# Ten normalisations in a fused eight-layer kernel: one reciprocal-root instruction per normalisation, and four of sixteen tiles moved from VectorE to ScalarE

## The reference

```python
def _layernorm(x, axis=-1, eps=1e-05):
    m = jnp.mean(x, axis=axis, keepdims=True)
    v = jnp.var(x, axis=axis, keepdims=True)
    return (x - m) / jnp.sqrt(v + eps)

x = x + _L0_attn_a_ref(_layernorm(x, axis=-1), ...)
x = x + _L0_ffn_ref(_layernorm(x, axis=-1), ...)
x = x + _L0_attn_b_ref(_layernorm(x, axis=-1), ...)
x = x + _L0_ffn_ref(_layernorm(x, axis=-1), ...)
x = x + _L1_attn_a_ref(_layernorm(x, axis=-1), ...)
x = x + _L1_ffn_ref(_layernorm(x, axis=-1), ...)
x = x + _L1_attn_b_ref(_layernorm(x, axis=-1), ...)
x = x + _L1_ffn_ref(_layernorm(x, axis=-1), ...)
```

## Time and profile before

| | |
|---|---|
| time, median of 3 runs | 1395.28 us (1394.18 to 1395.79) |
| the profiled execution's own time | 1395.96 us |
| its span, first to last instruction | 1394.1 us |
| PE busy (matmul) | 1048.9 us, 75% |
| DVE busy | 949.0 us, 68% |
| ACT busy | 509.3 us, 37% |
| POOL busy | 376.2 us, 27% |
| mean granted TensorE clock | 0.869 of full speed |

### The profile page before, as it was taken

The page is one execution under the profiler, slowest core; times in us unless marked ns, Lnnn a source line. Parts: engine busy times, 40 slices in busy tenths (PEclk is TensorE's granted clock), DMA queues, the critical chain, the costliest instruction groups (busy, mean ns, idle before and its releaser), DMA issues. The chain is left out here.

```text
span 1394.1 us, 17853 instructions
## 1 busy us (share of the span) xinstructions
PE 1048.9 (75%) x5802; PEld 544.4 (39%) x5802; DVE 949.0 (68%) x1953; ACT 509.3 (37%) x1034; POOL 376.2 (27%) x357
## 2 busy tenths in 40 slices
PE   4245999997599999957865766539994867539994
PEld 2112333343233333334544421316663444416663
DVE  6755998762699877447998799653336899653335
ACT  2403566776056677733101310103333411103333
POOL 2610000100100010012444344215662444415662
PEclk9657999999799999978995898559997887559997
DMA  3481000004400000271220111101112121001113
GB/s 93 112 93 26 2 1 1 1 2 69 71 2 1 1 1 2 31 203 41 68 61 0 39 46 53 30 12 36 41 45 78 38 65 33 22 21 35 43 43 110
DMA packets 43533, 58.24 MB, mean 42 GB/s; under 512 B 7630, under 2 KB 25878, under 8 KB 43438
## 3 DMA queue, kind: packets, MB, share of 16 engines
q1 hardware_dynamic: 38446, 46.79, 14.8%
q0 software_dynamic: 4992, 10.23, 2.6%
HBM read 42.95 MB, written 13.76 MB: 41 GB/s over the span
## 5 line engine op out<-in xcount | busy, mean ns | idle before, releaser
L578 DVE TENSOR_REDUCE mpart<-ps 128x1 f32<-128x512 f32 (+3 forms) x640 | 349.5, 603 | 114.8 <-PE ps L612 58.3
L674 ACT ACTIVATE arena<-ps 128x512 f32<-128x512 f32 (+3 forms) x640 | 296.2, 541 | 239.8 <-PE ps L630 163.8
L612 PE MATMUL ps<-arena 128*128 128x512 bf16 (+3 forms) x640 | 225.8, 365 | 49.9 <-PEq L388 18.3
L627 PE MATMUL ps<-arena 128*128 128x512 bf16 (+3 forms) x640 | 201.4, 350 | 14.1 <-DMA arena<-mrow 13.8
L910 POOL TENSOR_TENSOR arena<-arena 128x512 f32<-128x512 f32 x96 | 122.2, 1273 | 165.3 <-DVE arena L963 165.3
L612 PEld LDWEIGHTS ps<-arena 128*128 128x128 bf16 x640 | 62.3, 98 | 230.7 <-DVE mpart L578 146.6
L642 PE MATMUL ps<-arena,w 128*32 128x512 f32 (+3 forms) x1280 | 150.8, 543 | 0.4 <-ACT w L682 0.4
L1502 ACT ACTIVATE arena<-ps 128x512 f32<-128x512 f32 x78 | 46.6, 597 | 218.9 <-PE ps L1565 148.0
L1412 DVE COPY arena<-ps 128x128 f32<-128x128 f32 x78 | 22.8, 292 | 149.5 <-PE ps L1555 149.5
L949 DVE TENSOR_TENSOR arena<-arena 128x512 f32<-128x512 f32 x62 | 102.4, 1651 | 12.0 <-ACT arena L1016 4.6
L172 POOL TENSOR_TENSOR small<-small,neghalf 128x4 f32<-128x4 f32 x44 | 47.4, 1112 | 220.7 <-DVE small L159 220.7
(11 more groups left out here) (242 smaller groups left out, 1544.6 us busy)
## 6 DMA issues: line engine op xcount, KB each, us to landing
arena<-q_parts SPq DMA_DIRECT2D x12, 384.0 KB
w<-in_w SPq DMA_DIRECT2D x2, 2048.0 KB, 11.5
arena<-results SPq DMA_DIRECT2D x16, 256.0 KB, 4.5
arena<-g_v SPq DMA_DIRECT2D x15, 256.0 KB, 3.6
arena<-r_v SPq DMA_DIRECT2D x15, 256.0 KB, 3.6
arena<-l_v SPq DMA_DIRECT2D x15, 256.0 KB, 3.6
arena<-k_parts SPq DMA_DIRECT2D x8, 256.0 KB
tokens<-arena SPq DMA_DIRECT2D x8, 256.0 KB, 2.4
```

What stands on the lines that cost most here:

```text
L578: nc.vector.tensor_reduce(out=mpart[:, j, t, kc:kc + 1], in_=ps[:, S + m % DEPTH, 0:width], axis=AX.X, op=ALU.max).then_inc(ring_read, 1)
L612: ins = nc.tensor.matmul(out, Qs[b][:, j, (c * TPC + t) * P:(c * TPC + t + 1) * P], Ks[b][:, j, kc * CH:kc * CH + width], start=True, stop ...
L627: ins = nc.tensor.matmul(ps[:, ST + j, off:CH], Ks[b][:, j, kt * P:(kt + 1) * P], Qs[b][:, j, c * CH + off:(c + 1) * CH], start=True, stop ...
L674: nc.scalar.activation(probs[:, n % 2, j[0], off:CH], ps[:, ST + j[0], off:CH], ACT.Exp).then_inc(exp_done, 1)
```

## The change

All ten normalisations use one POOL instruction for the reciprocal roots of all their tiles (16 columns, or 32 for a1). Eight of them (all but a1 and l_o) are also "shared": DVE normalises groups 0 to 2, and ACT normalises the four tiles of group 3, as `Identity(scale * x + bias)` with scale = root and bias = -mean * root. For the bias DVE keeps the sum of the two half means in one more small instruction, and POOL makes two more instructions on four columns, each behind a wait. ACT does its four tiles ahead of its first copy. PE, and SP in the experts, wait for `act_normed` in place of the fourth `normed`.

```diff
         small = sb("small", [P, 10, 2 * NT])
-        neghalf = sb("neghalf", [P, NT])
+        neghalf = sb("neghalf", [P, 2 * NT])
...
-            def __init__(self, name, src, dst, n, eps, banks=(0, 1)):
-                self.src, self.dst, self.n, self.eps, self.banks = src, dst, n, eps, banks
+            def __init__(self, name, src, dst, n, eps, banks=(0, 1), shared=True):
+                self.src, self.dst, self.n, self.eps, self.banks, self.shared = src, dst, n, eps, banks, shared
+                self.by_act = n // 4 - 1 if shared else -1
+                self.bias_ready = sem(name + "_bias_ready")
+                self.act_normed = sem(name + "_act_normed")
...
                 nc.vector.tensor_scalar(mean, mean, 0.5, None, ALU.mult)
+                if self.shared:
+                    nc.vector.tensor_tensor(small[:, 6, 0:n], me, mo, ALU.add)
                 link(nc.vector.tensor_scalar(m2, m2, 1.0 / D, self.eps, ALU.mult, ALU.add))
                 nc.vector.scalar_tensor_tensor(out=var, in0=sq, scalar=0.25, in1=m2, op0=ALU.mult,
                                                op1=ALU.add).then_inc(self.var_ready, 1)
+                dve.wait_ge(self.rstd_ready, 1)
                 for g in range(n // 4):
-                    dve.wait_ge(self.rstd_ready, g + 1)
+                    if g == self.by_act:
+                        continue
                     for t in range(4 * g, 4 * g + 4):
...
             def gpsimd(self, pool):
                 pool.wait_ge(self.var_ready, 1)
-                for g in range(self.n // 4):
-                    nc.gpsimd.tensor_tensor(small[:, 5, 4 * g:4 * g + 4], small[:, 4, 4 * g:4 * g + 4],
-                                            neghalf[:, 0:4], ALU.pow).then_inc(self.rstd_ready, 1)
+                nc.gpsimd.tensor_tensor(small[:, 5, 0:self.n], small[:, 4, 0:self.n], neghalf[:, 0:self.n], ALU.pow).then_inc(self.rstd_ready, 1)
+                if self.shared:
+                    last = slice(self.n - 4, self.n)
+                    pool.wait_ge(self.rstd_ready, 1)
+                    nc.gpsimd.tensor_tensor(small[:, 7, last], small[:, 6, last], small[:, 5, last], ALU.mult).then_inc(self.bias_ready, 1)
+                    pool.wait_ge(self.bias_ready, 1)
+                    nc.gpsimd.tensor_scalar(small[:, 7, last], small[:, 7, last], -0.5, None, ALU.mult).then_inc(self.bias_ready, 1)
 
             def tensor(self, pe, groups=None):
                 for g in groups or range(self.n // 4):
-                    pe.wait_ge(self.normed, g + 1)
+                    if g == self.by_act:
+                        pe.wait_ge(self.act_normed, 1)
+                    else:
+                        pe.wait_ge(self.normed, g + 1)
...
             def scalar(self, act, groups=None):
+                if self.shared and (groups is None or 0 in groups):
+                    act.wait_ge(self.bias_ready, 2)
+                    for t in range(self.n - 4, self.n):
+                        ins = nc.scalar.activation(self.dst[:, t, :], self.src[:, t, :], ACT.Identity, bias=small[:, 7, t:t + 1],
+                                                   scale=small[:, 5, t:t + 1])
+                    ins.then_inc(self.act_normed, 1)
                 for g in groups or range(self.n // 4):
...
-                qkn_norm = Norm("a1", qk, qkn, 2 * NT, 1e-6, banks=(6, 7))
+                qkn_norm = Norm("a1", qk, qkn, 2 * NT, 1e-6, banks=(6, 7), shared=False)
...
-            norm = Norm(name + "_o", y.rearrange("p (t d) -> p t d", d=D), xn, NT, 1e-5)
+            norm = Norm(name + "_o", y.rearrange("p (t d) -> p t d", d=D), xn, NT, 1e-5, shared=False)
...
                     for g in range(NC):
-                        sp.wait_ge(norm.normed, g + 1)
+                        if g == norm.by_act:
+                            sp.wait_ge(norm.act_normed, 1)
+                        else:
+                            sp.wait_ge(norm.normed, g + 1)
```

## The result

The changed kernel takes 1415.6 us (median of 4 runs, 1411.59 to 1417.12) against 1395.53 us for the kernel before on the same chip (4 runs, 1394.18 to 1396.08): ratio 1.0141, 95% interval 1.0119 to 1.0163. The forecast was 1416.7 us. The profiled execution took 1417.12 us.

A forecast was written before the change was run, and what follows sets the result against it. The prediction took the wait for group 0 at each normalisation's head, with only the first root on the path, as the bound. Terms 0.8 + 6.1 + 3.8 + 2.0 + 1.6 + 2.4 + 4.7 = +21.4 on 1395.3 gave 1416.7 us, range 1408 to 1429.

The forecast's parts named there:

- The root's price: POOL's root heading each normalisation: straight line through one and four columns, 3.03 us for 16 columns, 5.69 for 32.
- Rival 1: POOL's root heading each normalisation: width is free, 16 or 32 columns cost 1.04 us; 1394.1 us, chance 0.12.
- rival 2: POOL's root: a column costs 0.25 us, 4.04 us for 16; +11.5 us more, 1428.2 us, chance 0.14.
- Rival 4: Clears of a0: DVE slips through ahead of them, -3 us in place of +2.4; 1411.3 us, chance 0.06.
- That it goes through to the end: Head of each normalisation: DVE starts 2.03 us later behind the 16-column root, and most stages move by about that.
- Linear layers and l_o: g, r, l: PE moves with group 0, 3 x 2.03 = +6.1 us; l_o: DVE scales after four groups, +2.03.
- f0 and f1: Channel mix: DVE's tiles end earlier, its mixes may be held behind subtractions; PE starts +0.8 us later each, +1.6 together.
- a0: POOL's clears again hold a DVE tile; projections start at 26.0, +2.4 us, bounds -3 and +3.
- a1: DVE starts 5.74 us behind the 32-column root instead of 1.05, +4.7 us, passed on through PE's wait for loads.
- m0, m1: Experts: sixteen transposes at DVE's pace start later, group 3 comes 0.1 us sooner; 2 x 1.9 = +3.8 us.
- ACT's share: ACT's four tiles take some 1.3 us, done 2.0 us behind the root, hidden by 0.4 us before its first copy.
- The sum: Whole kernel: all stage terms plus 0.8 us for the extra DVE instruction, +21.4 us, giving 1416.7 us.

The follow-up runs named there:

- e4: The changed kernel with every wide root computed twice and everything waiting for the second: 1452.19 us, ratio 1.0396 to the kernel before.
- e0: The changed kernel as it is, run again on another chip: 1421.28 us, ratio 1.0181 to the kernel before.
- e5: The kernel before, with POOL's four clears of a0 made to wait until DVE has normalised all sixteen tiles: 1389.06 us, ratio 0.9940.
- e2: The changed kernel with roots four columns at a time as before, ACT's four tiles kept, behind the last root: 1418.67 us, ratio 1.0151 to the kernel before.

## Why the prediction was right

**The root's price** was the step that decided, and it held: a straight line through two narrow shapes, 3.03 and 5.69 us, measured 2.93 and 5.46. Rival 1 (flat) and rival 2 (0.25 us a column: 4.04 us) are both refuted by one row. Rival 4 fell as well, since the clears of a0 again held one tile for 5.96 us. The GPSIMD Engine Reference of the Trainium skill (section "Elementwise — side-by-side cycle accounting") would have had twelve more columns for next to nothing. For the power this trace contradicts it: 2927 ns at sixteen columns against 1044 at four. For plain arithmetic it is near. The 2.6 cycles an element at 1.2 GHz of that section of the Trainium skill are about 2.2 ns, an estimate from its figures. POOL's product of four columns took 0.20 us (L182), and its subtraction of 512 took 3.11 / 3 = 1.04 us, so about 1.7 ns a column against 158 for the power.

**That it goes through to the end** held in the sum: e4 doubles the root and 30.9 of 32.5 us come out. For single stages it holds only together with TensorE's clock.

**Linear layers and l_o** (6.1 + 2.0 forecast, with 0.1 for the extra instruction here and there): measured g 2.4 to 2.6, r 2.3 to 2.4, l 1.7 to 2.0, l_o 2.1 to 2.3. DVE's start moved 1.92, a little less than forecast. The rest of g's is, by the windows above, TensorE's clock, a term that the sum lacked; r's second window shows the same (0.92 before, 0.77 changed).

**f0 and f1** (0.8 each): measured 0.95 and 0.94, and 0.48 and 0.81 in e0. The mechanism is as told: DVE out of the subtractions' way, its mixes of chunk 0 in it. But the fit of the number is in part luck. PE's start moved by 1.16 us in f0, in both traces of the changed kernel, against 0.8 forecast, and the clock gave some of it back: in the second 3 us of PE's products it stood at 0.86, and at 0.76 before.

**a0** (+2.4) was mis-sized. The mechanism held: three tiles, then one held for 5.96 us until the clears end (21.63), the rest behind it. The forecast had DVE's group 2 at 24.1 and two groups of 0.95 each behind it: "projections at 26.0". The clears ended 0.2 sooner than forecast, DVE was through at 15.23 + 8.60 = 23.83, and PE, which had started on group 0 at 21.93, reached group 2 at about that time without a wait. The projections began at 25.64, which is +2.0 on the clock of the trace and, since the root itself began 0.27 later than before, +1.7 behind the root. Of that 0.4 more did not reach a1: the 32 products took 11.51 us, 11.97 before, and in e0 10.49, where the whole stage came to +0.05. The windows of the first 3 us of the products (before, changed, e0) show where that lies:

```profile
23.65:26.65 3.00, 3.00 (x6) 1.68 (x6) 0.69 (x3) 1.16 (x3) 0.00 (x0) 1.00 0.09 1
25.64:28.64 3.00, 3.00 (x8) 1.69 (x8) 0.69 (x4) 1.33 (x3) 0.00 (x0) 1.00 0.01 0
25.20:28.20 3.00, 3.00 (x12) 1.81 (x11) 1.67 (x8) 2.10 (x6) 0.00 (x0) 1.00 0.01 0
```

The same 3 us hold 6, 8 and 12 products, and 11 in each trace's next 3 us. One by one the starts lie 0.64 us apart for the first few (four of them before, three in the changed kernel, none in e0) and then 0.32, half of that. Half the pace is what the half clock gives at the head of g, and the traces hold no clock record ahead of 26.63 (before), 27.71 (changed) and 24.98 (e0), so that the 1.00 in these rows says nothing of the time ahead of those. If the clock was at half until then, the loss is 1.5, 1.0 and 0 us (an estimate), and 11.97, 11.51 and 10.49 become the same 10.5. So what a0 kept back was most likely TensorE's clock; the granted clock itself is not shown there.

SBUF — State Buffer of the Trainium skill (the list under the diagram of the two sides) describes such a lock as lasting for one whole instruction. That the clears are what holds the tile e5 shows: with the clears behind, the tile of 5.96 us is gone. That it lasts for one instruction this trace contradicts: the held tile of the changed kernel starts at 15.75 and ends at 21.71, across all four clears, of which the longest takes 3.50 us.

**a1** (+4.7): 4.6 to 4.7 up to the wait for `k_parts`, in three traces. The forecast that this wait ends 7 us later came out (6.94), but 0.80 of it was a longer wait, which varies by more than 4 us between executions; that the number fits is chance in that part. That the 4.6 reach the end of the stage is argued, not shown: the scatter behind the wait is too large.

**m0, m1** (1.9 each): the logits start 1.69 us later behind m0's root (8.07 in place of 6.38); the stages came to +0.88 and +1.43, and +2.08 and +1.49 in e0. In m0 the clock again gave something back: the logits took 1.79 us at a granted clock of 0.82, and 2.42 at 0.58 before, so that the routing behind them began 1.06 later in both traces of the changed kernel. What the gathers behind that do to a us is not told apart.

**ACT's share** was costed at nothing, with 0.4 us of cover. It took 1.65 us, not 1.3, and used up the cover exactly. The forecast saw that it takes nothing and did not see how near that was: with the roots in fours the bias is ready 4.7 us behind the first root's start (3.6 in the changed kernel) while the first copy is wanted 2 us earlier, and the same four tiles cost 20 us (e2).

**The sum** came out to 0.4 us of the profiled stages (20.8 against 21.2 in the table), better than its terms deserve: they missed by 5 us in all, 1.1 too much in a0 and 1.6 in m0 and m1, 1.0 too little in a1 and 0.9 in g and r. The mechanism was right; that the total fits within 1.1 us is in part luck.

## What to carry to other kernels

Joining small instructions saves their starts on the engine that runs them, and delays the first consumer by all that it did not need yet. Look at who waits for the first piece, and read the price per element from shapes that the trace has: for the power on POOL 0.16 us a column made one root of sixteen 1.9 us longer than the first of four, at all nine normalisations of sixteen tiles. Work handed to an engine that executes in order belongs behind what the path wants from it: the same four tiles cost 1.5% ahead of two copies (1.0151) and 0.3% behind them (1.0027). And clears on POOL that start while DVE normalises can hold a single DVE tile for 6 us: moving four clears by one wait was worth 0.6% (0.9940, 0.9903 to 0.9976).

## What was not expected of the hardware

- Whether DVE is held beside POOL depends on what POOL runs. Beside clears a DVE tile of 0.33 us took 5.96, beside subtractions mixes of 0.74 took 1.5 each, but beside roots (sixteen tiles in 4.22 us) and beside eight weight copies (twelve in 3.16 us) DVE kept its pace. Which property of POOL's instruction decides is open.
- The same start delay costs more or less than itself by when TensorE's full clock comes behind it: g lost 2.64 and 2.41 for 1.92, but 4.32 for 4.9 in e4, and keeping PE busy in the gap brought g and l to +0.6 each, though not r. In the windows of g the longest idle time (12.26 us, e4) was followed by the earliest full clock, so a longer gap did not mean a longer time at half clock.
- The power on POOL is a straight line over a 32-fold width: 158 ns a column on a fixed 0.4 us (2927 - 16 x 158 = 399 ns, and 578 - 158 = 420 from the one-column root).
